# A graph-attention stage re-pipelined: scores turned to rows, one long maximum, rescaling on ScalarE, and the second table's scatters spread over six places

## The reference, cut to what matters

```python
feat_all = jnp.einsum('ni,rhid->rnhd', inputs, conv_weights)
feat_src_e = feat_all[edge_type, edge_src]
...
e = jax.nn.leaky_relu(el + er, negative_slope=LEAKY_SLOPE)
m = jax.ops.segment_max(e, edge_dst, num_segments=N_NODES)
ex = jnp.exp(e - m[edge_dst])
denom = jax.ops.segment_sum(ex, edge_dst, num_segments=N_NODES)
alpha = ex / denom[edge_dst]
h = jax.ops.segment_sum(alpha[..., None] * feat_src_e, edge_dst, num_segments=N_NODES)
```

## Time and profile before

| | us |
|---|---|
| median of three runs | 4170.91 (4170.29 to 4171.05) |
| the profiled execution, its time | 4176.44 |
| its span in the trace | 4174.7 |
| attention stage, first POOL gather to last `acc` | 704.2 to 2029.6 |
| first instruction of join, ln1, route, mixture, ln2 | 2030.4, 2057.5, 2094.6, 2130.1, 2352.6 |
| end of ln2's work | 2397 |
| an indirect scatter, issue to landing (page, part 6) | 2.1 |

### The profile page before, as it was taken

One profiled execution on the slowest core, in us unless ns is written; L12 is line 12 of the kernel. 1 busy time (PEld: TensorE's weight loads), 2 busy tenths in 40 slices (PEclk: granted clock), 3 DMA queues, 4 the chain that ended last, 5 costly groups with the idle time before them and its releaser, 6 DMA issues. The chain is left out here.

```text
span 4174.7 us, 73619 instructions
## 1 busy us (share of the span) xinstructions
PE 2928.3 (70%) x20296; PEld 2364.7 (57%) x20297; DVE 2177.3 (52%) x5961; ACT 1210.5 (29%) x3266; POOL 2277.2 (55%) x2336
## 2 busy tenths in 40 slices
PE   5199101777777777776379679999999864299990
PEld 1188101555555555555255358888888633288990
DVE  8411002877777777777743557777777444011112
ACT  1123000444444444444223223333333231022220
POOL 2777775777777777777240056666666200511115
PEclk8599655998998999999679789999999875599995
DMA  3344101222222222225100143333335501155533
GB/s 105 108 135 137 40 2 32 63 65 63 63 64 63 64 64 63 64 64 62 23 19 1 47 136 89 90 89 90 90 90 84 52 0 39 49 175 173 171 104 114
DMA packets 209214, 317.71 MB, mean 76 GB/s; under 512 B 63367, under 2 KB 150063, under 8 KB 208388
## 3 DMA queue, kind: packets, MB, share of 16 engines
q0 software_dynamic: 95008, 179.89, 19.9%
q1 hardware_dynamic: 103204, 127.24, 9.4%
q10 hardware_dynamic: 10944, 9.97, 0.7%
...
...
## 5 line engine op out<-in xcount | busy, mean ns | idle before, releaser
L1402 POOL DMA_INDIRECT conv_got<-xtab,conv_rowidx x588 | 565.8, 962 | 313.2 <-DVE conv_msg L1507 156.6
L806 POOL DMA_INDIRECT att_got<-feat,att_rowidx x588 | 573.2, 975 | 201.5 <-issue 150.2
L294 POOL DMA_INDIRECT table<-l0a_rec,l0a_addr x469 | 458.2, 977 | 216.7 <-issue 146.1
L1454 PE MATMUL conv_pf<-conv_wf,conv_act 128*128 128x256 f32 x2352 | 534.0, 380 | 0.2 <-DVE conv_filt L1502 0.2
L812 POOL DMA_INDIRECT table<-recs_rec,recs_addr x432 | 423.2, 980 | 131.6 <-issue 130.4
L1454 PEld LDWEIGHTS conv_pf<-conv_wf,conv_act 128*128 128x128 f32 x2352 | 447.6, 190 | 76.9 <-issue 0.8
L982 PE MATMUL att_pmax<-all_identb,att_away 128*128 128x512 bf16 x588 | 261.1, 444 | 203.9 <-DVE att_elo L901 203.2
L863 DVE TENSOR_REDUCE att_tmax<-att_pmax 128x4 f32<-128x512 f32 x588 | 373.8, 680 | 31.1 <-PE att_pmax L986 27.6
L986 PE MATMUL att_pmax<-all_identb,att_ehi 128*128 128x128 bf16 x2352 | 383.6, 242 | 0.0
L986 PE MATMUL att_pmax<-all_identb,att_elo 128*128 128x128 bf16 x2352 | 383.3, 242 | 0.0
L1420 ACT ACTIVATE conv_act<-conv_p,conv_bf 128x512 f32<-128x512 f32 x294 | 186.2, 684 | 552.1 <-PE conv_p L1446 552.1
...
...
## 6 DMA issues: line engine op xcount, KB each, us to landing
...
table<-l0a_rec,l0a_addr POOLq DMA_INDIRECT x469
table<-recs_rec,recs_addr POOLq DMA_INDIRECT x469, 2.1
```

Source lines behind the costliest of these rows:

```text
L294: self.nc.gpsimd.indirect_dma_start(out=self.table, out_offset=bass.IndirectOffsetOnAxis(ap=self.addrs[:, j:j + 1], axis=0), in_=self.recs ...
L806: nc.gpsimd.indirect_dma_start(out=got[g % 3][:, k, :], out_offset=None, in_=feat, in_offset=bass.IndirectOffsetOnAxis(ap=rowidx[:, g * K ...
L1402: nc.gpsimd.indirect_dma_start(out=got[g % 3][:, k, :], out_offset=None, in_=xtab, in_offset=bass.IndirectOffsetOnAxis(ap=rowidx[:, g * K ...
L1454: ins = nc.tensor.matmul(pf[b][:, k, :], act1[s3][:, h, (2 * b + k) * P:(2 * b + k + 1) * P], wf2[:, h, :], start=(h == 0), stop=(h == 1))
```

## The change

- **Pipeline depth.** Four buffers and groups up to four steps back (`DEPTH`, `SLOTS` = 4) in place of three. `below` stays two steps back; `ex`, the products and the sums move to three steps back, `acc` to four. `f` has two buffers, `pmax` and `psum` one.
- **Scores to rows.** DVE writes both parts of the scores into `spread`, PE turns it (`pE`, four transposes to 32 rows), ACT copies it (`eT`, bfloat16). `pmax` of a block is then two matmuls of 512 columns, and one DVE reduce over 2048 elements gives the maximum of the group.
- **Rescaling on ACT.** ACT computes `shrunk` = `acc` x `keep` (four instructions of 65 elements); DVE adds `psum` in one instruction of 260 elements.
- **Sums in two parts.** Three of the four blocks are summed ahead of `pme`, the fourth behind it.
- **Types at once.** `typ` is made for all edges before the first step (4704 elements), and the memset of `acc` moves behind the row indices.
- **Scatters.** `attend` issues one or two scatters a group (214 in all). The other 255 go to `join_attention` (12), `ln1` (26), `route` (24), `mixture` (167, from 37) and `ln2` (26).

```diff
-ROUND = 3
-COLS1 = ROUND * (ET // K - 3), EJ - ROUND * (ET // K - 3)
-assert sum(COLS0) == EJ == sum(COLS1) and COLS1[1] > 0
+COLS1 = ET // K - 4 + (ET // K - 4) // 2, 12, 26, 24, 167, 26
...
-    GROUPS, SLOTS = ET // K, 3
+    GROUPS, SLOTS, DEPTH = ET // K, 4, 4
...
+    ROWS = 2 * K * HEADS
...
+        typ = s.sb("typ", [P, ET, RELS], BF16)
...
+        spread = [s.sb(f"spread{u}", [P, HEADS, ROWS], BF16) for u in four]
+        eT = [s.sb(f"eT{u}", [ROWS, HEADS, P], BF16) for u in range(2)]
...
+        f = [s.sb(f"f{u}", [P, K, HEADS, H1]) for u in range(2)]
...
+        shrunk = s.sb("shrunk", [P, HEADS, H1])
+        select = s.sb("select", [ROWS, K], BF16)
+        pmax = s.ps("pmax", [P, K, HEADS, P])
...
+            sends = [0 if g < SLOTS else 1 + g % 2 for g in range(GROUPS)]
...
+                u = g % SLOTS
                 if g >= SLOTS:
-                    pool.wait_ge(f_ready, g - 2)
-                    pool.wait_ge(last_ready, (g - 2) * LAST)
+                    pool.wait_ge(f_ready, g - SLOTS + 1)
+                    pool.wait_ge(last_ready, (g - SLOTS + 1) * LAST)
...
+                wait_positive(pool, sent[u], 16 * sum(sends[u:g:SLOTS]))
+                for i in range(sum(sends[:g]), sum(sends[:g + 1])):
                     nc.gpsimd.indirect_dma_start(
                         out=table1, out_offset=bass.IndirectOffsetOnAxis(ap=addr1[:, i:i + 1], axis=0),
-                        in_=rec1[:, i, :], in_offset=None).then_inc(sent[g % 3], 16)
...
-            v.memset(acc[:, :, :, :], 0.0).then_inc(prep, 1)
-            v.memset(mrun[:, :, :], -BIG).then_inc(prep, 1)
             dve.wait_ge(loaded, 16)
             v.tensor_copy(rowidx[:, :], recs[:, :, 0]).then_inc(prep, 1)
+            v.tensor_copy(erparts[:, 0], er[:, :, :]).then_inc(ready, 1)
+            v.memset(acc[:, :, :, :], 0.0).then_inc(ready, 1)
+            v.memset(mrun[:, :, :], -BIG).then_inc(ready, 1)
...
+            v.tensor_tensor(typ[:, :, :], bcast(c["ramp"][:, 0:RELS], [[0, ET], [1, RELS]]),
+                            recs[:, :, 2].unsqueeze(2).broadcast_to([P, ET, RELS]), ALU.is_equal).then_inc(ready, 1)
...
+                s1, s2, s3, s4 = ((u - d) % SLOTS for d in (1, 2, 3, 4))
+                if 0 in parts:
+                    wait_positive(dve, sum_ready, t - 3)
+                    wait_positive(dve, away_ready, t - 3)
+                    dest = recs[:, bass.ds(t * K, K), 1]
+                    v.tensor_tensor(oh[u][:, :, :], bcast(c["ramp"][:, 0:P], [[0, K], [1, P]]),
+                                    dest.unsqueeze(2).broadcast_to([P, K, P]), ALU.is_equal).then_inc(oh_ready, 1)
...
+                    g = t - 3
+                    dve.wait_ge(ex_ready, g + 1)
+                    wait_positive(dve, sum_ready, g - 1)
+                    n = ON_DVE
+                    v.tensor_tensor(f[(u - 3) % 2][:, 0:n, :, 0:HD], got[s3][:, 0:n, 0:D].rearrange("p k (h d) -> p k h d", h=HEADS),
+                                    ex[:, 0:n, :].unsqueeze(3).broadcast_to([P, n, HEADS, HD]), ALU.mult).then_inc(f_ready, 1)
+                if 4 in parts:
+                    bin4 = bin_of(dve, t - 4)
+                if 1 in parts:
...
+                    dve.wait_ge(er_ready, g + 1)
+                    v.tensor_tensor(ert[:, :, :, :], per[:, :, 0:RELS * HEADS].rearrange("p k (r h) -> p k h r", r=RELS),
+                                    typ[:, bass.ds(g * K, K), :].unsqueeze(2).broadcast_to([P, K, HEADS, RELS]), ALU.mult).then_inc(picked, 1)
...
+                    v.tensor_reduce(ers[:, :, :], ert[:, :, :, :], AX.X, ALU.add).then_inc(ers_ready, 1)
+                    dve.wait_ge(got_s[s1], ((i + 1) if u else i) * 16 * K)
+                    dve.wait_ge(ers_ready, g + 1)
+                    v.tensor_tensor(z[:, :, :], ers[:, :, :], got[s1][:, :, D:FW], ALU.add).then_inc(z_ready, 1)
+                    dve.wait_ge(z_ready, g + 1)
...
+                    v.tensor_copy(at[0], e[s1][:, :, :]).then_inc(high, 1)
+                    dve.wait_ge(high, g + 1)
+                    v.tensor_tensor(at[1], e[s1][:, :, :], at[0], ALU.subtract).then_inc(e_ready, 1)
...
-                        dve.wait_ge(max_ready, g * K + k + 1)
-                        count(v.tensor_reduce(tmax[:, k, :], pmax[k][:, :, :], AX.X, ALU.max))
...
+                    dve.wait_ge(max_ready, g + 1)
+                    v.tensor_reduce(tmax[:, :], pmax[:, :, :, :].rearrange("p k h e -> p h k e"), AX.XY, ALU.max).then_inc(tmax_ready, 1)
...
+                if 4 in parts:
+                    g = t - 4
+                    dve.wait_ge(sum_ready, g + 1)
+                    dve.wait_ge(shrunk_ready, (g + 1) * HEADS)
+                    v.tensor_tensor(flat(flat(acc[:, bass.ds(bin4, 1), :, :], "p a b c -> p a (b c)")), flat(shrunk[:, :, :]), psum[:, 0:HEADS * H1], ALU.add).then_inc(acc_done, 1)
                 if 2 in parts:
+                    g = t - 2
                     dve.wait_ge(me_ready, g + 1)
                     wait_positive(dve, col_ready, g)
                     v.tensor_tensor(below[:, :, :], e[s2][:, :, :], pme[:, :, 0:HEADS], ALU.subtract).then_inc(below_ready, 1)
...
-                    dve.wait_ge(sum_ready, t - 2)
-                    wait_positive(dve, acc_done, t - 3)
-                    for h in range(HEADS):
-                        shrink(h)
...
+                def products(k):
+                    for h in range(HEADS):
+                        nc.scalar.activation(f[(u - 3) % 2][:, k, h, 0:HD], got[s3][:, k, h * HD:(h + 1) * HD], ACT.Copy,
+                                             scale=ex[:, k, h:h + 1]).then_inc(last_ready, 1)
...
+                    products(ON_DVE)
+                if 4 in parts:
+                    bin4 = bin_of(act, t - 4)
...
+                    nc.scalar.activation(flat(ohT[u][:, :, :]), pT[:, 0:K * P], ACT.Identity, bias=c["ones"][:, 0:1], scale=1.0 / BIG).then_inc(ohT_ready, 1)
+                if 1 in parts:
+                    g = t - 1
+                    act.wait_ge(spread_turned, g + 1)
+                    wait_positive(act, max_ready, g - 1)
+                    nc.scalar.activation(flat(eT[(u - 1) % 2][:, :, :]), pE[:, 0:HEADS * P], ACT.Copy).then_inc(eT_ready, 1)
+                if 3 in parts:
+                    for k in range(ON_DVE + 1, K):
+                        products(k)
+                if 4 in parts:
+                    g = t - 4
+                    wait_positive(act, acc_done, g)
+                    act.wait_ge(keep_ready, g + 1)
+                    for h in range(HEADS):
+                        nc.scalar.activation(shrunk[:, h, :], flat(acc[:, bass.ds(bin4, 1), h, :]), ACT.Copy,
+                                             scale=keep[s4][:, h:h + 1]).then_inc(shrunk_ready, 1)
...
-                        nc.tensor.matmul(pmax[k][:, :, :], away[s1][:, k, :], bcast(c["identb"][:, :], [[0, HEADS], [1, P]]),
-                                         start=True, stop=False, skip_group_check=True)
-                        for h in range(HEADS):
-                            for part in (ehi, elo):
-                                ins = nc.tensor.matmul(pmax[k][:, h, :], part[s1][:, k, h:h + 1].broadcast_to([P, P]), c["identb"][:, :],
-                                                       start=False, stop=(part is elo), skip_group_check=True)
...
+                def sums(g, ks):
+                    for k in ks:
+                        if k >= ON_DVE:
+                            pe.wait_ge(last_ready, g * LAST + (k - ON_DVE + 1) * HEADS)
+                        ins = nc.tensor.matmul(psum[:, 0:HEADS * H1], oh[s3][:, k, :], flat(f[(u - 3) % 2][:, k, :, :]), start=(k == 0), stop=(k == K - 1))
+                    return ins
...
+                    bin0 = bin_of(pe, t)
+                if 1 in parts:
+                    g = t - 1
+                    pe.wait_ge(e_ready, g + 1)
+                    wait_positive(pe, eT_ready, g)
+                    for h in range(HEADS):
+                        ins = nc.tensor.transpose(pE[:, h * P:(h + 1) * P], spread[s1][:, h, :], c["identb"][:, :])
+                    ins.then_inc(spread_turned, 1)
...
+                if 3 in parts:
+                    g = t - 3
+                    wait_positive(pe, acc_done, g)
+                    pe.wait_ge(col_ready, g + 1)
+                    pe.wait_ge(f_ready, g + 1)
+                    sums(g, range(ON_DVE + 1))
                 if 2 in parts:
...
+                    pe.wait_ge(m_ready, g + 1)
+                    wait_positive(pe, below_ready, g)
+                        for n in range(2):
+                            ins = nc.tensor.matmul(pme[:, k, 0:HEADS], ohT[s2][:, k, :], mparts[:, n, :], start=(n == 0), stop=(n == 1))
+                    ins.then_inc(me_ready, 1)
+                if 3 in parts:
+                    sums(t - 3, range(ON_DVE + 1, K)).then_inc(sum_ready, 1)
+                if 1 in parts:
+                    g = t - 1
```

(23 more changed lines are left out.)

243 lines of the change are left out of this document (83 added, 160 removed).

## The result

The changed kernel takes 4655.9 us (median of four runs, 4652.2 to 4659.4) against 4171.0 for the one before, timed beside it: ratio 1.116, 95% interval 1.114 to 1.118. The direction was forecast, the size was not: +485 us in place of +170, and outside the range.

What follows compares the result with a forecast made beforehand. GpSimd's seven DMAs a group were taken to bound the kernel. After the change, 9.8 us a step (9.1 plus 0.7 for the clock) gave attention +135, mixture +19.5, join +15.6: +170, 4341 us, range 4195 to 4420.

Steps and rivals of the forecast that it cites:

- What bounds before: Attention before the change: GpSimd's seven indirect DMAs of 1.28 us a group set the step of 8.97 us.
- GpSimd's part: Attention: 4 gathers and on average 1.5 scatters a group remain, 7.05 us in place of 8.97.
- The ring: Attention: a closed chain of waits through TensorE, VectorE and ACT, once round per step, sets the step at 9.10 us.
- four links: Attention: sums wait for `acc`, `pme` for three blocks' sums, next `oh` for the last sum, `acc` for `shrunk`.
- The sum of the legs: Attention: times from the sums through `pme`, `oh`, scores, `eT`, `shrunk` and `acc` to the next sums, 9.10 us.
- The clock: TensorE in attention: idle 2.7 us a step, 0.6 falls to half clock at 1.15 us, +0.7 us a step.
- the end of the range: Attention's slow end: a fall of TensorE's clock in each step at 1.4 us, 10.5 us a step.
- Rival B: Attention: the chain of waits holds and the clock adds nothing, 9.1 us a step, 4240 us; chance 0.20.
- its rule: TensorE: the skill warns only of idle gaps longer than 2.7 us, so the clock costs nothing.
- Attention's ends: Attention's start and drain: about +11.5 us at the start, first full step near 741, drain 22 us.
- mixture: Stage `mixture`: its 167 scatters outlast the stage's work, +19.5 us.
- join: Stage `join`: VectorE's long additions hold up a scatter, between 0 and +15.6 us, the latter taken.

Runs made afterwards that it cites:

- e5: The attention loops of the kernel before, with its scatters spread as in the changed kernel: 3962 us.
- e2: The changed kernel with the block of `pme` put ahead of the first sums on TensorE: 4568 us.
- e8: The changed kernel with 24 transposes of the identity on TensorE ahead of its wait for `acc_done` in every step: 4313 us.
- e1: The changed kernel with 32 transposes of the identity on TensorE ahead of its wait for `acc_done` in every step: 4325 us.

## Why the prediction was wrong in its size

- **What bounds before, and GpSimd's part: right.** 5.5 DMAs a group give 7.18 us a step in e5 (forecast for GpSimd 7.05).
- **The ring and its four links: right.** All its waits stand in every step, e2 took out 0.58 us, about `pme`'s own time, and the second `psum` bank opens it. The sum of the legs, 9.10 us, is 9.34 in e8 at full clock; `oh` and `f`, with the bin loads behind them, were 0.4 short, the rest nearly cancels. VectorE's wait for `pme` in that step is 1.85 us, the 1.9 of the forecast.
- **The clock: the step that failed.** I took 0.6 falls a step at 1.15 us, +0.7, and for the end of the range one fall a step at 1.4 us. It is 11.92 - 9.34 = +2.6 us, for 143 steps 370 us. The number of falls was about right, one in two steps; each costs 5.2 us. Two things in that price were wrong. The length of a low stretch, 3.5 us, was taken from before and is 17 us here, over the sums of both steps. And only the six passes of the sums were charged. The 512-column matmuls of `pmax`, which I costed at nothing "while the clock is full", start 0.32 us apart at full and 0.54 at half clock, 4.3 us in place of 2.6 for the eight; `pT` stands behind them, and so `ohT` and all that follows it. In the step of 12.72 us, 1.9 of the 3.4 us over 9.34 lie between the sums and `oh`, and 1.4 in the wait of `eT` behind `ohT`. e1 and e8 show that TensorE's standing brings this on; that the stretch is so long because the wait is itself a link of the ring, and comes again at half clock, is argued and not shown.
- **Rival B and its rule.** By the rule in the Trainium skill that the prediction quotes ("TensorE: Matmul & The Clock Gate"; its section is "Why this matters for your kernels"), standing for 2.7 us costs nothing. The trace disagrees, with 0.64 and falls after 1.7 us of standing. The same page (A second HAM failure mode: psum-queue depth-cycling) tells of a kernel whose clock goes up and down by small waits between groups of matmuls, which I had not weighed; e1 agrees with it: with the waits filled the clock is 0.94.
- **Attention's ends: nearly right.** The rows give the sixth `oh` at 753.2; the forecast 741 for the fifth was 742.7. The end lies at 2473.7, where 763 + 143 x 11.92 = 2467.6.
- **mixture: +23.4 us for +19.5.** The stage is 245.9 us long instead of 222.5. The scatters end at 2826.55 and ln2 begins at 2833.48, 6.9 us later, where I had 2.1 for the landing and nothing for the stage's end.
- **join: +13 us for +15.6,** 40.1 instead of 27.1. Three operations each held one scatter, where the prediction had one scatter of some 25 us. The Trainium skill ("SBUF — State Buffer", SBUF: two separate sides) describes a lock for the whole instruction; the first of the three scatters ends at 2484.92, 0.82 us after the operation's 2484.10, which agrees as far as the scatter goes. VectorE's next operation starts at 2484.13, before that scatter's end, and takes its 8.16 us all the same, so no wait of VectorE shows. ln1 and route: 0, as forecast.
- **Sum.** With the step at its measured 11.92 us the forecast would have been 4341 + 143 x (11.92 - 9.8) = 4644 us.
